# Float16 token halves turned by DMA transposes instead of TensorE, from the third attention batch on

## What is computed

```
z = layernorm(x)                      # per token, 8 batches x 1024 tokens x 128 features
scores = (z @ Qw) @ (z @ Kw).T / sqrt(128) + causal mask
x = x + softmax(scores) @ (z @ Vw)
x = x + 0.5 * ffn(layernorm(x))       # before and after the attention
```

## Time and profile before

| | |
|---|---|
| median of 3 runs | 674.8 us (672.57 to 675.33) |
| the profiled execution, its own time | 675.56 us |
| its span | 673.7 us |
| busy in the span: PE, DVE, ACT, POOL | 636.5, 550.5, 555.6, 521.6 us |
| mean granted TensorE clock | 0.982 of full |
| DMA queue q1 (SP): share of 16 engines' span | 64.5% |
| attention, 263 to 434 us: PE, DVE, ACT, POOL busy | 159.1, 126.5, 139.8, 103.5 us of 171 |

### The profile page before, as it was taken

How to read it: one execution, slowest core, us unless ns; L and a number is a source line. 1 busy time by engine, 2 the same in 40 slices (tenths; PEclk the granted TensorE clock), 3 DMA queues, 4 the chain that set the end, 5 groups by cost and what they waited for, 6 DMA issues and landing times.

```text
span 673.7 us, 15214 instructions
## 1 busy us (share of the span) xinstructions
PE 636.5 (94%) x3395; PEld 494.1 (73%) x3395; DVE 550.5 (82%) x2558; ACT 555.6 (82%) x1191; POOL 521.6 (77%) x411
## 2 busy tenths in 40 slices
PE   4689999999999999699999999999999999999997
PEld 3457777777777777578888877677777777777775
DVE  5888999898898896567777689878999988998863
ACT  3478888888988999878889877679888898887975
POOL 3378999889988987756656656559989899998876
PEclk9589999999999999899999999999999999999999
DMA  9865677875677770344464452965678887777773
GB/s 245 197 146 130 128 161 152 167 151 127 146 150 157 153 154 1 65 91 75 77 102 83 80 100 56 211 135 130 150 172 174 173 170 159 146 173 165 165 167 82
DMA packets 107801, 92.05 MB, mean 137 GB/s; under 512 B 59488, under 2 KB 73456, under 8 KB 107760
## 3 DMA queue, kind: packets, MB, share of 16 engines
q1 hardware_dynamic: 105552, 91.00, 64.5%
q10 hardware_dynamic: 2208, 0.59, 0.4%
HBM read 72.70 MB, written 5.24 MB: 116 GB/s over the span
## 4 chain that ended last, share of the span: by engine, by line
PE 76%; DVE 8%; ACT 5%; issue 4%; POOL 3%; DMA 3%; POOLq 0%; DVEq 0%; ACTq 0%; SPq 0%
PE psum L1386 20%; PE psum L1387 19%; PE psum L1388 19%; PE psum L1459 4%; PE psum L1417 2%; PE psum L1471 2%; DVE w_raw L1268 2%; PE psum L1647 1%; POOL shared L551 1%; PE psum L1433 1%; DMA wb<-scratch 1%; PE psum L1631 1%; PE psum L1632 1%; PE psum L1633 1%; PE psum L1604 1%
## 5 line engine op out<-in xcount | busy, mean ns | idle before, releaser
L459 POOL TENSOR_TENSOR shared_r<-shared,shared_r 128x512 fp32r<-128x512 f32 x256 | 326.2, 1294 | 48.9 <-ACT shared L649 46.3
L1119 DVE SCALAR_TENSOR_TENSOR s_sb<-psum,wb 128x512 f32<-128x512 f32 x256 | 175.5, 687 | 46.3 <-PE psum L1388 22.6
L649 ACT ACTIVATE shared<-s_sb 128x512 f32<-128x512 f32 x288 | 177.9, 619 | 24.1 <-DVE s_sb L1119 24.0
L648 ACT ACTIVATE shared_r<-s_sb 128x512 fp32r<-128x512 f32 x256 | 159.8, 624 | 35.7 <-DVE s_sb L1119 33.5
L1386 PE MATMUL psum<-x_hi,w_hi 128*128 128x512 f32 x288 | 126.6, 439 | 1.4 <-issue 0.9
L1386 PE MATMUL psum<-shared_r,w_hi 128*128 128x512 f32 x256 | 115.2, 450 | 0.9 <-POOL shared_r L459 0.7
L1388 PE MATMUL psum<-x_hi,w_lo 128*128 128x512 f32 x288 | 114.3, 397 | 0.0
L1387 PE MATMUL psum<-x_lo,w_hi 128*128 128x512 f32 x288 | 114.2, 396 | 0.0
L1387 PE MATMUL psum<-shared_r,w_hi 128*128 128x512 f32 x256 | 101.7, 397 | 0.0
L1388 PE MATMUL psum<-shared_r,w_lo 128*128 128x512 f32 x256 | 101.1, 395 | 0.0
L551 POOL TENSOR_TENSOR shared<-s_sb,shared 128x1024 f16<-128x1024 f32 (+3 forms) x32 | 56.7, 1771 | 46.2 <-ACT shared L579 46.2
(11 more groups left out here) (169 smaller groups left out, 1369.7 us busy)
## 6 DMA issues: line engine op xcount, KB each, us to landing
wb<-scratch SPq DMA_DIRECT2D x128, 512.0 KB, 8.0
out<-x_sb SPq DMA_DIRECT2D x16, 256.0 KB, 9.9
x_sb<-in_L_attn_x SPq DMA_DIRECT2D x4, 256.0 KB, 6.1
scratch<-wT SPq DMA_DIRECT2D x32, 32.0 KB, 1.9
w_raw<-in_L_ffn_W ACTq DMA_DIRECT2D x1, 512.0 KB, 5.9
w_raw<-in_L_ffn_W SPq DMA_DIRECT2D x1, 512.0 KB, 6.6
wb<-shared SPq DMA_TRANSPOSE x32, 4.0
w_raw<-in_L_ffn_Ws ACTq DMA_DIRECT2D x1, 64.0 KB, 8.4
```

Of the source, the lines that this page charges most:

```text
L459: nc.gpsimd.tensor_tensor(g_lo[:, j % RING, :], g_f[:, j % RING, :], g_hi[:, j % RING, :].bitcast(F32), ALU.subtract).then_inc(F.glo_done, 1)
L648: nc.scalar.activation(g_hi[:, j % RING, :], s_sb[:, j % RING, :], ACT.Square)
L649: nc.scalar.activation(g_f[:, j % RING, :], s_sb[:, j % RING, :], ACT.Square).then_inc(F.sq_done, 1)
L1119: ins = nc.vector.scalar_tensor_tensor(s_, h_, 0.0, wb[:, u, c, :], ALU.max, ALU.mult)
```

## The change

PE's `z_transpose` is left only for batches 0 and 1. For batches 2 to 7 SP issues two DMA transposes per batch (`tokens_transpose`), one for each half of the tokens. Each turns eight 128 x 128 float16 blocks (four tiles, high and low half) of `zn16` into a new tile `zT16`. ACT's `z_hi_copy` and DVE's `z_lo_part` then read that tile: the high part is a copy of the turned high half, the low part a copy of the turned low half, in place of a subtraction from PSUM.

Orders and buffers change with it. `zn16` has three batches of room. POOL makes half 0 of the float16 tokens of b+1 at the head of batch b, ahead of `attention_inv` and `prob_lo(b, 7)`, and half 1 behind `prob_lo(b, 7)`; before, they stood behind the third and the second `prob_lo`. ACT's two copies stand behind the exponentials of steps 1 and 2, DVE's two behind the row maxima of steps 1 and 2. On SP the two issues for batch b+1 stand ahead of `prob_transpose(b, 7)` and of `prob_transpose(b, 6)`.

```
@@ SP
+            def tokens_transpose(b, half):
+                sp.wait_ge(AT.z16lo_done[half], b + 1)
+                wait(sp, AT.zlo_done[half], b)
+                sp.dma_start_transpose(zT16[:, half].rearrange("p a (k q) -> p (a k) q", q=P),
+                                       zn16_own[:, b % 3, half].rearrange("p a k d -> p (a k d)")).then_inc(AT.zT_in[half], 16)
...
                         for t in LATE:
+                            if t in LATE[:2] and 0 < b < B - 1:
+                                tokens_transpose(b + 1, LATE.index(t))
                             prob_transpose(b, t)
@@ POOL
                 def z16_halves(b, half):
                     pool.wait_ge(A.zn_done[half], b + 1)
-                    wait(pool, A.pair_done[PAIRS[1]], b - 1)
+                    wait(pool, A.pair_done[PAIRS[1]], b - 2)
...
                 for b in range(B):
+                    if b + 1 < B:
+                        z16_halves(b + 1, 0)
                     if b + 2 < B:
                         attention_inv(b + 2)
                     for t in LATE:
                         prob_lo(b, t)
-                        if t == LATE[1] and b + 1 < B:
+                        if t == LATE[0] and b + 1 < B:
                             z16_halves(b + 1, 1)
-                        if t == LATE[2] and b + 1 < B:
-                            z16_halves(b + 1, 0)
                         start_behind(b, t)
@@ ACT
                 def z_hi_copy(b, half, src):
-                    sc.wait_ge(A.t_done[half], b + 1)
-                    copy(z_hi[:, b % UN, half * 512:half * 512 + 512], src).then_inc(A.zhi_done[half], 1)
+                    if b < 2:
+                        sc.wait_ge(A.t_done[half], b + 1)
+                    else:
+                        sc.wait_ge(A.zT_in[half], 16 * (b - 1))
+                        src = zT16[:, half, 0]
+                    copy(z_hi[b % UN][:, half * 512:half * 512 + 512], src).then_inc(A.zhi_done[half], 1)
...
-                            if b + 1 < B and s in (0, 2) and b > 0:
-                                z_hi_copy(b + 1, s // 2, prep_ps)
                             exp(b, s)
+                            if b + 1 < B and s in (1, 2) and b > 0:
+                                z_hi_copy(b + 1, s - 1, prep_ps)
@@ DVE
+                    if b < 2:
+                        tt(z_lo[b % UN][:, cs], src, f32(z_hi[b % UN][:, cs]), ALU.subtract).then_inc(A.zlo_done[half], 1)
+                    else:
+                        nc.vector.tensor_copy(z_lo[b % UN][:, cs], zT16[:, half, 1]).then_inc(A.zlo_done[half], 1)
...
-                            if b + 1 < B and s in (0, 2) and (b, s) != (0, 0):
-                                z_lo_part(b + 1, s // 2, prep_ps)
+                            if b + 1 < B and s in ((1, 2) if b > 0 else (2,)):
+                                z_lo_part(b + 1, s - 1, prep_ps)
@@ PE
                             if s == 0:
-                                if new:
+                                if b == 0:
                                     wait(pe, A.qlo_done[0], b + 1)
                                     z_transpose(b + 1, 0, prep_ps)
...
-                            if s == 2 and new:
+                            if s == 2 and b == 0:
                                 pe.wait_ge(A.zlo_done[0], b + 2)
                                 z_transpose(b + 1, 1, prep_ps)
...
                             if s == 4 and new:
+                                pe.wait_ge(A.qlo_done[0], b + 1)
                                 q_product(b + 1, 1, prep_ps)
```

More of the change, by code:

```diff
@@ L94, in __init__ @@
         self.t_done = halves("t_done")
+        self.zT_in = halves("zT_in")
         self.zhi_done = halves("zhi_done")
@@ L234, in zn, with zn16 @@
             return zn_homes[:, b % 3 if half == 0 else 2 if b == 0 else 3]
-        z_hi = sb("z_hi", [P, UN, S], F32R)
-        z_lo = sb("z_lo", [P, UN, S], F32R)
+        z_own = sb("z_own", [P, 2, S], F32R)
+        z_hi = [z_own[:, 0], shared_r[:, 2 * S:3 * S]]
+        z_lo = [z_own[:, 1], shared_r[:, 3 * S:4 * S]]
         q_hi = [x_hi[:].rearrange("p u n -> p (u n)"), shared_r[:, 0:S]]
         q_lo = [x_lo[:].rearrange("p u n -> p (u n)"), shared_r[:, S:2 * S]]
-        zn16_own = sb("zn16", [P, 2, 2, QT, D], F16)
-        zn16 = [zn16_own[:, 0], zn16_own[:, 1]]
+        zn16_own = sb("zn16", [P, 3, 2, 2, HQ, D], F16)
+        zT16 = sb("zT16", [P, 2, 2, HQ * P], F16)
+        def zn16(b, part, key):
+            return zn16_own[:, b % 3, key // HQ, part, key % HQ, :]
         rows = w_raw[:, HQ * HQ * P:HQ * HQ * P + 14 * QT].rearrange("p (a t) -> p a t", t=QT)
@@ L332, in tokens_free @@
                 wait(eng, AT.mix_done, done)
-            wait(eng, AT.t_done[half], done)
+            wait(eng, AT.t_done[half], min(done, 2))
             wait(eng, AT.z16lo_done[half], done)
@@ L539, in z16_halves @@
                     pool.wait_ge(A.zn_done[half], b + 1)
-                    wait(pool, A.pair_done[PAIRS[1]], b - 1)
-                    ts = slice(half * HQ, (half + 1) * HQ)
-                    nc.gpsimd.tensor_copy(zn16[b % 2][:, 0, ts, :], zn(b, half)).then_inc(A.z16hi_done[half], 1)
+                    wait(pool, A.pair_done[PAIRS[1]], b - 2)
+                    hi, lo = (zn16_own[:, b % 3, half, part] for part in range(2))
+                    nc.gpsimd.tensor_copy(hi, zn(b, half)).then_inc(A.z16hi_done[half], 1)
                     pool.wait_ge(A.z16hi_done[half], b + 1)
-                    nc.gpsimd.tensor_tensor(zn16[b % 2][:, 1, ts, :], zn(b, half), zn16[b % 2][:, 0, ts, :],
+                    nc.gpsimd.tensor_tensor(lo, zn(b, half), hi,
                                             ALU.subtract).then_inc(A.z16lo_done[half], 1)
@@ L1253, in z_lo_part @@
                     cs = slice(half * 512, half * 512 + 512)
-                    tt(z_lo[:, b % UN, cs], src, f32(z_hi[:, b % UN, cs]), ALU.subtract).then_inc(A.zlo_done[half], 1)
+                    if b < 2:
+                        tt(z_lo[b % UN][:, cs], src, f32(z_hi[b % UN][:, cs]), ALU.subtract).then_inc(A.zlo_done[half], 1)
+                    else:
+                        nc.vector.tensor_copy(z_lo[b % UN][:, cs], zT16[:, half, 1]).then_inc(A.zlo_done[half], 1)
                 def q_lo_part(b, half, src):
@@ L1577, in q_product @@
                     cs = slice(half * 512, half * 512 + 512)
-                    split3(dst, m_hi[:], m_lo[:], z_hi[:, b % UN, cs], z_lo[:, b % UN, cs]).then_inc(A.q_done[half], 1)
+                    split3(dst, m_hi[:], m_lo[:], z_hi[b % UN][:, cs], z_lo[b % UN][:, cs]).then_inc(A.q_done[half], 1)
                 def score(b, s):
@@ L1595, in score @@
                             continue
-                        split3(dst[:, c0:c1], q_hi[u][:, qs], q_lo[u][:, qs], z_hi[:, u, c0:c1], z_lo[:, u, c0:c1], stop=(c1 < w))
+                        split3(dst[:, c0:c1], q_hi[u][:, qs], q_lo[u][:, qs], z_hi[u][:, c0:c1], z_lo[u][:, c0:c1], stop=(c1 < w))
                     mm(dst[:, t * P:w], identb[:], maskb[:], start=False, stop=True).then_inc(A.sc_done, 1)
@@ L1630, in pair @@
                         out_, p_hi, p_lo = u_ps[:, q0:end], pT16[:, k, 0, q0:end], pT16[:, k, 1, q0:end]
-                        mm(out_, zn16[b % 2][:, 0, k, :], p_hi, start=(k == 0), stop=False)
-                        mm(out_, zn16[b % 2][:, 0, k, :], p_lo, start=False, stop=False)
-                        ins = mm(out_, zn16[b % 2][:, 1, k, :], p_hi, start=False, stop=(k == first + 1))
+                        mm(out_, zn16(b, 0, k), p_hi, start=(k == 0), stop=False)
+                        mm(out_, zn16(b, 0, k), p_lo, start=False, stop=False)
+                        ins = mm(out_, zn16(b, 1, k), p_hi, start=False, stop=(k == first + 1))
                     if k1 == first + 2:
```

## The result

| | before | after |
|---|---|---|
| median of 4 runs each | 674.24 us | 746.28 us (743.47 to 747.91) |
| ratio | | 1.1075, interval 1.1044 to 1.1106 |
| profiled execution / its span | 675.56 / 673.7 us | 747.91 / 746.1 us |
| PE, DVE, ACT, POOL busy | 636.5, 550.5, 555.6, 521.6 us | 650.2, 545.2, 558.4, 521.2 us |
| mean granted TensorE clock | 0.982 | 0.933 |

A forecast was written before the change was run, and what follows sets the result against it. A steady batch was taken as bound by PE, with ACT 1.65 us behind. 675.56 plus 69.9 us for the late landings and 3 for the clock gave 748.5, forecast as 748 us, range 724 to 766.

The forecast's parts named there:

- The chain to the landings: Batches 1 to 6, POOL's halves, DMA landings and copies up to step 4's exponentials: 142.7 us against 72.8 before.
- A: Start of the exponentials of step 7 of batch b-1, from which the forecast counts each batch's delays.
- The estimate of 2.6 us: DMA transpose of eight blocks by 2.0 us fixed plus bytes over 436 GB/s; would lower the sum some 6 us.
- the second wait: ACT's wait for half 1, queued behind half 0's copy: about 7 us a batch, after about 2.5 for half 0.
- nothing shrinks: ACT works without a gap from step 4 to the next A, 8.8 us, so each batch's delay adds to the next.
- the 3 us charged for the clock: PE at half clock after idle gaps, charged 0.5 us a batch in six batches, bounds 0 and 17.
- Six stretches of some 6 us: Half clock expected on PE after each of six gaps, with 2.9 us of PE work lost each.
- rival 1: Landings come before ACT and DVE ask; PE's 5.3 us and part of ACT's waits go: 669 us, chance 0.04.
- The two moves that the prediction did call free: POOL's earlier work on half 0 in batch 0 and the third `zn16` buffer were said to cost nothing.
- PE's 5.3 us: Two groups of token transposes taken off PE in batches 2 to 7, 12 x 0.44 us, counted as nothing.

The follow-up runs named there:

- experiment 3: Changed kernel with DVE's `mean(b+2)` moved ahead of its `z_lo_part` in step 1; 737.8 us, ratio 1.096.
- experiment 4: Changed kernel with half 1's float16 tokens made on POOL right behind half 0's and both transposes issued there; 710.46 us, ratio 1.0555.
- Experiment 11: Changed kernel with PE's two gaps in each of batches 1 to 6 filled by products nobody reads; 745.48 us, ratio 1.1058.
- experiment 5: Changed kernel with both halves' float16 tokens made and their DMA transposes issued a batch ahead; 693.85 us, ratio 1.0309.
- experiment 2: Changed kernel with PE's transposes back and copies in their old places, keeping POOL's order, third buffer and moved tiles; 674.11 us, ratio 1.0002.
- experiment 1: Changed kernel with only the DMA route undone: PE's transposes back, new copy places, POOL order and buffers kept; 695.12 us, ratio 1.0335.
- experiment 7: As experiment 6, but DVE copies the low part with a reduction over groups of one element instead of a cast; 675.43 us, ratio 1.0023.
- experiment 9: As experiment 7, with half 0 made and turned behind `prob_lo(b, 4)`, copied at step 4, batch 1's halves later in batch 0; 674.63 us, ratio 1.0018.
- experiment 6: As experiment 5, but ACT's and DVE's copies in the places of the kernel before, half 1 first; 681.48 us, ratio 1.0105.
- experiment 10: As experiment 9, with DVE's cast in place of the reduction; 676.31 us, ratio 1.0040.

## Why the prediction was right, and what it had wrong

**The chain to the landings** was right step by step. In the trace of after the six distances from A to the exponentials of step 4 are 22.2, 22.8, 24.5, 24.5, 23.3 and 22.7 us, together 140.1 against 142.7 forecast and 72.8 before. The landing of eight blocks alone was 3.1 us, as worked out from the earlier trace rows, behind the sixteen-block one 3.5 to 3.7 instead of 3.9; the cast took 0.43 us instead of 0.5. The estimate of 2.6 us that the prediction set beside it comes from the Trainium skill, "DMA: Bandwidth & Descriptors", Anatomy of one DMA, a part on DMAs that GpSimd issues; for these, which SP issues, the measured 3.1 us decides. That `mean` and `attention_inv` stand in the chain is shown by experiment 3, that the second wait stands behind the first by experiment 4.

**From step 4 to the next A** "nothing shrinks" held: 51.2 us in six batches against 47.7. The 3.5 us more come near the 3 us charged for the clock, but not in the way that they were charged, 0.5 us in every batch: they stand in batches 1, 3 and 4 alone, 0.9, 1.4 and 1.4 us. Experiment 11 takes them away in 1 and 3, so there they are the clock's; in 4 that stays open. And there was more half clock than forecast. Six stretches of some 6 us are 36 us; a mean clock of 0.80 over 191.2 us, taken as time at 0.50 and at 1.00, makes an estimate of 76 us. That the price still came near was in part luck. By the Trainium skill, "TensorE: Matmul & The Clock Gate", Part 1, the engine falls to 1.2 GHz when it idles and comes back when it is kept busy; the windows above agree in kind, 0.50 behind the gaps and 0.90 to 1.00 in the last two windows of the filled kernel.

**Right in the sum, with one price missing from the account.** The prediction followed every queue, and so its sum holds what the copies' new places cost, in the words "only then DVE's row maximum of step 3, queued behind `z_lo_part`". But it has no price for them, and rival 1, "the landings come before ACT and DVE ask for them", puts them at nothing: 669 us. With the landings a batch ahead the changed kernel still takes 694 us (experiment 5). The two moves that the prediction did call free, POOL's earlier work and the third buffer, were free (experiment 2). By experiments 1 and 2 the loss of 72 us is some 23 for the copies' new places and, as what remains, some 50 for the late transposes; experiment 5, which takes the lateness away and leaves the places, gives 52 for it. The copies moved one step back, which looks like more time for the DMA, and tied DVE's row maxima to ACT's exponentials.

**PE's 5.3 us** were rightly counted at nothing for the changed kernel. With the copies in their old places, the landings in time and the casts out of POOL's way, 2.3 and 2.6 us of them come in batches 1 to 6 (experiments 7 and 9), and the time is level with the kernel before. Why no more comes, and whether the rest could, stays open. No version beat the kernel before.

## What to carry to other kernels

A transfer that takes the place of an engine's step must be followed from its producer: here the step on PE was 0.44 us, and its replacement could start only when another engine's queue had come to it, twice in a row. A copy that stood in front of an instruction which waits anyway was free; the same copies behind it cost 23 us, since the other engine's next work hung on them. PE, busy for 97% of the six batches, gave back only half of what was taken off it, with ACT at 85%. That the two hand work to each other all the time is the likely reason, and isn't shown.

## What the runs showed of the hardware that I had not expected

A DVE cast of 128x512 from float16 in SBUF takes 0.43 us while POOL is idle, and up to 2.38 us when it starts inside a POOL subtraction (experiment 6). In experiments 6 and 10 twenty casts began inside a `prob_lo` or a cast of POOL, and each ended 0.27 to 0.29 us after that. One that began inside POOL's `inv`, 1.01 us on 128x4, was not held: 0.42 us; why isn't shown. A reduction of the same operand takes 0.68 us, more than the cast alone, and isn't held up (experiment 7). Nor was the subtraction from PSUM of the kernel before, 0.68 to 0.69 us in all sixteen cases, twelve of them beside a POOL instruction. The Trainium skill, "SBUF — State Buffer", Who interferes with whom, says it: "DVE in 2-port perf mode (`2×_2P`, `4×_2P`) contends with GpSimd", the later one blocks until the other is done, a cast can be in such a mode, and a `tensor_reduce` never contends on trn2. No view names the mode of an instruction; the times agree, 2.22 us beside a `prob_lo` against 0.43 alone, and 0.68 for every reduction. So a faster instruction was, in its place, the slower one.
